# Weights split once in the first stage, with the order of the gap and of the end rearranged

## The reference

```python
x = x + layernorm(attn(layernorm(x)))
x = x + layernorm(ffn(layernorm(x)))

def attn(X):
    h = layernorm(X) * ln_w + ln_b
    Q, K, V = split(h @ W_in + b_in, 3)
    Q, K = rope_half(Q), rope_half(K)
    A = sum(K / norm(K) * V, over the tokens of a batch)
    return (A[:, None, :] * Q) @ W_out + b_out + X

def ffn(x):                      # 8 experts, H = 256; shared SH = 512
    gates = softmax of the top 2 of x @ gate_w
    routed = sum over e of gates[e] * (gelu(x @ w1[e] + b1[e]) @ w2[e] + b2[e])
    return routed + gelu(x @ shared_w1 + shared_b1) @ shared_w2 + shared_b2
```

## Time and profile before

| what | value |
|---|---|
| median of 3 runs | 1030.75 us (1030.19 to 1032.58) |
| the profiled execution | 1027.98 us |
| its span, first to last instruction | 1025.8 us |
| TensorE busy | 896.8 us, 87% |
| VectorE, ACT, GpSimd busy | 628.3, 442.0, 404.4 us |
| mean granted TensorE clock | 0.95 |
| first stage | about 0 to 316 us |
| second stage | 316 to 540 us |
| gap | 540 to 657 us |
| routed tiles | 657 to 910 us |
| last stage | 910 to 1026 us |

### The profile page before, as it was taken

How to read it: one execution, slowest core, us unless ns; L and a number is a source line. 1 busy time by engine, 2 the same in 40 slices (tenths; PEclk the granted TensorE clock), 3 DMA queues, 4 the chain that set the end, 5 groups by cost and what they waited for, 6 DMA issues and landing times.

```text
span 1025.8 us, 14729 instructions
## 1 busy us (share of the span) xinstructions
PE 896.8 (87%) x4562; PEld 739.3 (72%) x4562; DVE 628.3 (61%) x1356; ACT 442.0 (43%) x830; POOL 404.4 (39%) x337
## 2 busy tenths in 40 slices
PE   1999999999997699999999748499999999969883
PEld 1877787787785467777778537488988988857662
DVE  5656766676664775656665587366665666655653
ACT  4134233433423124122242645366666666653462
POOL 3356446545631400000000000277677777730464
PEclk9999999999998889999999878799999999989886
DMA  9122644545337568645424650678778878789496
GB/s 314 45 81 105 244 143 161 188 158 200 135 144 306 190 239 312 227 165 215 154 83 169 215 151 32 238 144 149 140 147 163 154 146 149 147 176 350 62 160 107
DMA packets 78074, 174.68 MB, mean 170 GB/s; under 512 B 10841, under 2 KB 19289, under 8 KB 73137
## 3 DMA queue, kind: packets, MB, share of 16 engines
q1 hardware_dynamic: 52096, 124.60, 33.6%
q0 software_dynamic: 20592, 45.96, 25.1%
q10 hardware_dynamic: 5312, 3.18, 1.3%
HBM read 103.68 MB, written 80.53 MB: 180 GB/s over the span
## 4 chain that ended last, share of the span: by engine, by line
PE 70%; DVE 11%; issue 7%; ACT 4%; POOL 3%; DMA 2%; SPq 1%; POOLq 0%; ACTq 0%; DVEq 0%
PE bank L1434 12%; PE bank L1435 12%; PE bank L1436 12%; PE bank L1626 3%; PE bank L1628 3%; PE bank L1627 3%; PE bank L1643 3%; PE bank L1645 3%; PE bank L1644 3%; PE bank L1613 3%; PE bank L1429 3%; POOL out L1413 2%; DVE we L1061 2%; PE bank L1635 2%; ACT hb L535 1%
## 5 line engine op out<-in xcount | busy, mean ns | idle before, releaser
L1385 POOL DMA_INDIRECT f_scratch<-ro,dst x71 | 113.2, 1595 | 48.7 <-SPq L513 23.2
L1377 POOL DMA_INDIRECT xr<-n_scratch,ids x72 | 71.1, 987 | 90.9 <-issue 65.6
L1434 PE MATMUL bank<-wkv_hi,h_hi 128*128 128x512 f32 x256 | 101.1, 395 | 3.8 <-issue 3.8
L1436 PE MATMUL bank<-wkv_hi,h_lo 128*128 128x512 f32 x256 | 100.7, 393 | 0.0
L1435 PE MATMUL bank<-wkv_lo,h_hi 128*128 128x512 f32 x256 | 100.6, 393 | 0.0
L1188 DVE TENSOR_TENSOR ro<-bank,b2b 128x512 f32<-128x512 f32 x71 | 49.1, 692 | 70.3 <-PE bank L1645 70.3
L1626 PE MATMUL bank<-we,x_hi 128*128 x284 | 86.4, 304 | 0.0
L1628 PE MATMUL bank<-we,x_lo 128*128 x284 | 80.7, 284 | 0.0
L1627 PE MATMUL bank<-we,x_hi 128*128 x284 | 80.6, 284 | 0.0
L544 ACT ACTIVATE sq<-kb 128x512 f32<-128x512 f32 x32 | 20.3, 633 | 134.2 <-DVE kb L845 134.2
L1344 POOL TENSOR_TENSOR zr<-zv,half 128x4 f32<-128x4 f32 x8 | 8.1, 1009 | 137.7 <-DVE zv L961 137.7
(11 more groups left out here) (232 smaller groups left out, 2514.2 us busy)
## 6 DMA issues: line engine op xcount, KB each, us to landing
xg<-in_X SPq DMA_DIRECT2D x16, 1024.0 KB, 9.1
q_scratch<-qh SPq DMA_DIRECT2D x8, 1024.0 KB, 3.9
q_scratch<-qb SPq DMA_DIRECT2D x8, 1024.0 KB, 7.1
expert_scratch<-in_w SPq DMA_DIRECT2D x16, 512.0 KB, 7.1
q_hi<-q_scratch SPq DMA_DIRECT2D x8, 1024.0 KB, 4.7
q_lo<-q_scratch SPq DMA_DIRECT2D x8, 1024.0 KB, 6.9
out<-z SPq DMA_DIRECT2D x8, 1024.0 KB, 5.1
n_scratch<-n SPq DMA_DIRECT2D x8, 1024.0 KB, 6.4
```

The lines of the kernel that those rows point to most:

```text
L1377: pool.indirect_dma_start(xr[u][:, :], None, n3_dram, bass.IndirectOffsetOnAxis(ids[:, i:i + 1], 0)).then_inc(row_in[u], 16)
L1385: pool.indirect_dma_start(f_dram, bass.IndirectOffsetOnAxis(dst[:, i:i + 1], 0), ro[i % NRO][:, :], None, compute_op=ALU.add).then_inc(r_s ...
L1434: pe.matmul(dst, hi(k), w_hi(k), start=(k == 0), stop=False)
L1436: last = pe.matmul(dst, lo(k), w_hi(k), start=False, stop=(k == KD - 1 and not more))
```

## The change

- All weights are split in the first stage. `units` lists 20 pieces of 128x1024: two for each expert, two halves for each shared weight. Four are done in each of groups 1 to 5. SP loads a piece into the buffer of its lo part (`load_unit`, three buffer pairs), ACT makes hi (`unit_hi`), VectorE lo (`unit_lo`), and SP stores both (`store_unit`). The copies DRAM to DRAM go. ACT and VectorE spread the four over the group, two in the k and v part, two around q.
- The bias row `bo` is split in group 0, and the bias product takes the constant `ones_f` instead of `bo_one`. `W_out` is loaded behind the last unit, and batch 0 is scaled at g = 6 instead of 4.
- `split_s` at s = 0 goes; the shared weights are loaded as two parts, those of w1 ahead of s = 0 and those of w2 in it.
- EARLY becomes (0, 2, 4, 6, 7), LATE (1, 3, 5). `fill` starts at s = 1 and has seven entries, so that `shared_h(6)` runs in s = 7.
- For s = 7 VectorE does nothing else between `z_moments` and `x2_shift` but the x2 tiles and one `hs_lo_part`; `top2(6)` comes behind the `hs_lo_part` of group 6.
- In the gap no expert is split. The weights are loaded in two parts, some already in s = 3 and 4. `shared_o(7)` runs twice ahead of the one-hot loop and twice in it. `f_out` of group 6 has four buffers of its own.
- The loads of n3 of the first late group and of the shared w1's hi part wait for eight turns of routed tiles. The first late group's four turns have four banks and run among the last routed tiles. `late_h(0)` does the products with hi weights of all four columns first, then those with lo weights, whose transfer is issued behind the last routed product.
- The early groups' f tiles are measured and normalized earlier, f is loaded in another order, each group with its own semaphore; in the last stage nc parts come ahead of statistics. The last late group's x2 is loaded (`x2c`), added by VectorE, and stored by SP without accumulation. One gather and one x turn fewer.

The core of the diff:

```diff
-EARLY = (1, 3, 5, 6, 7)
+EARLY = (0, 2, 4, 6, 7)
...
+        UW = KD * H
+        UG = 4
+        units = [(e, i, 0) for e in range(E) for i in range(2)] + [(E + i, 0, h) for i in range(2) for h in range(2)]
+        UB = 3
...
-        fill = {2 + i: (("h", "o")[i % 2], EARLY[i // 2]) for i in range(6)}
+        fill = {1 + i: (("h", "o")[i % 2], EARLY[i // 2]) for i in range(7)}
...
-        measured = beside((0, 0, 0, 0, 1, 1, 1, 1, 2, 2, 2, 2, 1, 1, 0, 0, 2, 2, 1, 1, 0, 0, 0, 0))
-        normed_in = beside((0, 0, 0, 0, 0, 0, 0, 0, 0, 1, 1, 1, 2, 2, 2, 2, 1, 1, 1, 1, 2, 1, 1, 1))
+        measured = beside((0, 0, 2, 2, 1, 1, 1, 1, 2, 2, 2, 2, 1, 1, 1, 1) + (0,) * 8)
+        normed_in = beside((0, 0, 0, 0, 0, 0, 2, 2, 0, 0, 1, 1, 2, 2, 2, 2, 1, 1, 1, 1, 1, 1, 0, 0))
...
+            def load_unit(u):
+                if u >= len(units):
+                    return
+                if u >= UB:
+                    sp.wait_ge(w_stored[u % UB], 32 * (u // UB))
+                w, k = unit_in(u)
+                sp.dma_start(w_lo[u % UB][:, :].bitcast(F32).rearrange("p (k h) -> p k h", k=k), w).then_inc(raw_w_in[u % UB], 16)
+
+            def store_unit(u):
+                sp.wait_ge(unit_split, u + 1)
+                for c, w in ((0, w_hi), (1, w_lo)):
+                    sp.dma_start(unit_out(u, c), w[u % UB][:, :].bitcast(F32)).then_inc(w_stored[u % UB], 16)
...
             for g in range(NG):
+                u = UG * (g - 1)
+                with_units = 0 <= u < len(units)
                 sp.wait_ge(h_normed, g + 1)
                 load_x(g + 2)
+                if with_units:
+                    store_unit(u)
+                    load_unit(u + 2)
                 if g >= 1:
                     store_q(g - 1)
+                if with_units:
+                    store_unit(u + 1)
+                    load_unit(u + 3)
                 if g + 1 < NG:
                     sp.wait_ge(k_rotated, GT * (g + 1))
                     load_rt(g + 1)
+                if with_units:
+                    store_unit(u + 2)
+                    load_unit(u + 4)
+                if g + 1 < NG:
                     sp.wait_ge(q_rotated, g + 1)
                     load_rf(g + 1)
-                if 1 <= g <= 4:
-                    copy_expert(2 * g - 2)
-                    copy_expert(2 * g - 1)
...
+                if with_units:
+                    store_unit(u + 3)
+                    load_unit(u + 5)
...
-            for n, g in enumerate(f_loads):
-                sp.dma_start(f[g][:, :, :], f_groups[g]).then_inc(f_in[n // 2], 16)
-            sp.wait_ge(stored, 16 * NT)
+            load_f(EARLY[0])
+            load_f(EARLY[1])
+            load_f(LATE[0])
+            load_f(EARLY[2])
+            load_f(EARLY[3])
+            load_n3(2)
+            load_f(LATE[1])
+            load_f(EARLY[4])
+            load_f(LATE[2])
+            sp.dma_start(x2c[:, :, :], out_groups[LATE[2]]).then_inc(f_in[LATE[2]], 16)
+            for j in range(GT):
+                sp.wait_ge(y_added, j + 1)
+                sp.dma_start(out_tiles[GT * LATE[2] + j], f[LATE[2]][:, j, :]).then_inc(late_stored, 16)
...
+            def unit_hi(u):
+                act.wait_ge(raw_w_in[u % UB], 16 * (u // UB + 1))
+                if u >= UB:
+                    act.wait_ge(w_stored[u % UB], 32 * (u // UB))
+                act.activation(w_hi[u % UB][:, :], w_lo[u % UB][:, :].bitcast(F32), ACT.Copy).then_inc(unit_hi_done, 1)
...
+            def unit_lo(g, j):
+                u = UG * (g - 1) + j
+                if 0 <= u < len(units):
+                    dve.wait_ge(unit_hi_done, u + 1)
+                    dve.tensor_tensor(w_lo[u % UB][:, :], w_lo[u % UB][:, :].bitcast(F32), w_hi[u % UB][:, :].bitcast(F32), ALU.subtract)\
+                       .then_inc(unit_split, 1)
...
                 kv_prod(g, 0)
+                unit_lo(g, 0)
                 v_tile(g, 1)
...
                 kv_prod(g, 2)
+                unit_lo(g, 1)
                 v_tile(g, 3)
                 kv_prod(g, 3)
+                unit_lo(g, 2)
                 rotate_q(g)
                 if g + 2 < NG:
                     front_stats(g + 2)
-                if g == GB + 1:
+                unit_lo(g, 3)
+                if g == GB + 2:
                     wo_lo_parts(0)
...
-            expert_lo((5, 1, 2, 6))
...
-                x_turn(i + 1, 1 - u, (i + 1) % NX)
+                if i < PRE:
+                    x_turn(i + 1, 1 - u, (i + 1) % NX)
+                else:
+                    pe.wait_ge(n3c_in[0], 16)
+                    pe.wait_ge(xt_free, PRE)
+                    late_turn_part(0, 0)
                 h_of(i, u, e)
+                if i == PRE:
+                    late_turn_part(0, 1)
                 o_of(i - 1, 1 - u, e_before)
+            pe.wait_ge(th_free, 2 + PRE)
+            late_turn_part(0, 2)
             h_turn(PRE, PRE % 2)
             o_of(PRE, PRE % 2, e)
+            late_turn_part(0, 3)
```

## The result

The changed kernel takes 993.36 us (median of 4 runs, 993.01 to 995.51) where the kernel before, run beside it, takes 1030.47 us: a ratio of 0.9641, 95% interval 0.9621 to 0.9661. It is faster by 37 us. The forecast was 971 us, 59.5 us faster, with a range up to 992: the direction is right, the gain is 1.6 times too large, and the time lies just outside the range.

What follows compares the result with a forecast made beforehand. TensorE bounds first-stage groups and routed tiles; gains lie in its waits between. First stage +4, second-stage start -18, its groups -2, routing -20, late groups -24 make -60 us: 968 profiled, 971 median; range 958 to 984, with A, B, D 955 to 992.

Steps and rivals of the forecast that it cites:

- The new wait for q(1): Start of the second stage: TensorE waits about 3 us for `load_q(1)`, then three `attend` follow.
- The wait ahead of `late_o(0)`: Last stage: VectorE measures two tiles of the first f before `hc_lo(0,3)`; a new wait of some 6 us.
- rival C: First stage: a unit's chain on three buffers sets the pace; +74 instead of +4 us, 1041 us; chance 0.03.
- D: Rival, routing gap: the splits were not on the path; -6 instead of -20 us, 985 us; chance 0.05.
- its own signs: Groups 1 to 5 at 37 us, first `n3` turn about 347, first mark about 591, `late_o(1)` waits under 2 us.
- Rival B: Late stage stays bound by transfers: -10 instead of -24 us, 985 us; chance 0.08.
- From there two waits shrink ... TensorE ends at about 994: Last stage: waits of 4.4 us on `nc_lo` and 3.45 us on `hc_lo` shrink; TensorE's end gains 15 us.
- The groups of the second stage keep their period.: Second stage: group period unchanged, shared products only start one group earlier; -2 us for the `n_lo` wait.
- start of the second stage: From the first stage's end to the first `n3` turn: -18 us, or -14 if q(1) lands 4 us late.
- 0.8 us a group: First stage: first unit's subtraction delays the last k tile and `hb`; five groups, +4 us.
- Rival A: First stage: each subtraction collides with its GpSimd neighbour; some +14 instead of +4 us, 981 us; chance 0.14.
- I count 22: Routing: the marks' loop over 16 batches falls from 29 to 22 us, -7 us.

Runs made afterwards that it cites:

- e3: Changed kernel with two VectorE statistics moved, so none of f is measured ahead of `hc_lo(0,3)`: ratio 0.9642 to the kernel before, last stage 88.3 us.
- e11: Changed kernel with output products of the second and third late group waiting for each `hc_lo` quarter separately: ratio 0.9628 to the kernel before.
- e7: Changed kernel with e3's start, plus ACT normalizations and two VectorE statistics moved behind the gelu: ratio 0.9648 to the kernel before.
- e1: Changed kernel with the stores of zeros issued one group earlier: 984.66 us, ratio 0.9607 to the kernel before.
- e4: Changed kernel without the units' 20 ACT copies and 20 VectorE subtractions, all transfers kept: ratio 0.9586 to the kernel before.
- e8: Changed kernel with the second unit's subtraction left out in each of five groups: ratio 0.9625 to the kernel before.
- e5: Changed kernel with the first two subtractions moved behind the last k/v product, each unit's load ahead of the previous store: ratio 0.9724 to the kernel before.
- e6: Changed kernel with `load_q(1)` issued ten us earlier, ahead of the last q store: ratio 0.9667 to the kernel before.
- a1: Changed kernel repeated without edit, on the same chip as a repeat of the kernel before: span 990.5 us, routed tiles 257.5 us.

## Why the prediction was off

*What held.* The bias row and the splits gone from the gap: marks begin 9.9 us earlier within the gap (forecast 9), the gathers take 3.9 us less (4). The tail: 9.2 us (9). The new wait for q(1), 3.7 us (3). The wait ahead of `late_o(0)`: 7.7 us (6), and `late_h(1)` starts 36.4 us behind the last routed product (36). Rivals C and D did not come: ACT waits for no raw weights, and the marks follow at once. The routed tiles are unchanged. Of its own signs the forecast missed three: the first n3 turn came at 353.2 us instead of 347, the first mark at 600.4 instead of 591, and the wait ahead of `late_o(1)` was 2.14 us, over its 2. Rival B came halfway: last stage and tail gave 16.6 us, between its 10 and the forecast's 24, with f's landing ahead of `late_o(0)` and that of `c_lo` behind it (e3); but the larger part of what is missing is no transfer.

*The step that failed most: "From there two waits shrink ... TensorE ends at about 994".* It counted the last stage's second half nearly free of waits and of slow clock. From `late_h(1)` to the end it took 54.9 us instead of 48. There were 4.4 us of waits for `hc_lo`, 0.7 for `hsc` and slow products behind each. The last quarter's gelu, copy and subtraction (0.67 + 0.63 + 0.69 us) come behind the last `late_h` product, and nothing of the group's own can run beside them as long as TensorE asks for all four quarters. e11 shows this for 4.4 of the 6.9 us; e7 rules out the order of the normalizations; beside the 2.5 that stay, e11's rows have waits for `hsc` (1.7 us) and `f` (1.1). With the first half right, the stage gave 7.4 us of 15.

*"The groups of the second stage keep their period."* They did not: 36.1 us once instead of 30.3. I followed the shared products when they moved a group earlier, but not their stores, and so not past the four transfers of zeros that stand in SyncE's queue in that group. e1 prices it at 6 us.

*The slow clock behind a wait that I had predicted.* I put in 3 us for q(1) but let the three `attend` behind it run at full clock (10.1 us); they took 12.96 us. Term: start of the second stage, -12.7 instead of -16.

*First stage: "0.8 us a group".* Measured 1.5, and 7 us in all with e4. The chain that the forecast priced, first subtraction, last k tile, `hb`, is there, but TensorE's wait for `hb` grows by 0.3 us only (0.43 to 0.72). What the forecast did not count is the wait of 1.1 us for `qb`, most of it due to the second unit's subtraction, ahead of the last v tile (e8: 0.8 us a group). Rival A described the collision and named `h_lo`, but priced four equal ones at 14 us in all. The costly one is the second unit's, and it reaches `h_lo` through `rn`, `acc` and `prod`. By the Trainium skill (SBUF — State Buffer, Who interferes with whom) a VectorE instruction with two SBUF inputs contends with a GpSimd instruction that reads SBUF. By that rule, the trace agrees: even the 128 x 1 `rn` grows from 0.55 to 1.37 us, and in e5 `acc` and `h_lo` grow although VectorE was idle there before.

*The marks' loop: "I count 22".* It took 25.3 us on VectorE (600.4 to 625.7): two output products stand ahead of the first marks on TensorE, which is ready for them only at 606.6, and the last five batches run at the lower clock (12 products in 3.03 us where 12 take 1.42). Read from the timeline, not tried.

The differences of measured and forecast, in the order of the table's rows: 2.8 (the first two), 3.3, 4.3, 2.2, 0.1, then 5.5 for the routed tiles, which before and after share on one chip, 7.6, and -0.2 for the tail: 25.7 us before rounding, the 60 less the 34.3.

*Two slips in the prediction's working.* The units of a group are four transfers of 0.5 MB in and eight out, not "8 transfers to SBUF"; the 6.3 MB are right. And rival C would decide earlier than it says: four units on three buffers take 36 us as soon as a chain takes 27, that is at 12.4 us a landing and not at 17. The landings were far below it, 5.3 us for the loads of the experts' units and 2.6 and 4.1 for their stores (medians).

## What to carry to other kernels

An idle stretch of VectorE is free for work with two SBUF inputs only if GpSimd is idle too: ask what GpSimd does there before moving such work into it. When work moves a step earlier in a hand-written order, walk each of its transfers past everything that its queue holds in the new place. Count slow products behind every wait of some 3 us on TensorE, also one that you predict yourself, and as a risk behind one of 2 us; a wait that ends in another one of the same length has won nothing (e6). And read an experiment's gain from the groups that it changes, not from a stretch that ends in something else (e8).

## What the runs showed of the hardware

The same instructions of the routed tiles took 253.2 to 254.3 us on one chip and 257.5 to 258.3 us on three others, and those of the kernel before 252.6 us once and 257.0 once; 10 to 14 late `hc` against 1 or 2 go with it. A 4 us difference between two profiles of this kernel in that stage is not evidence of a change.

A short wait brings the lower level of the clock at one time and not at another. Behind 3.29 us (e6) the turn's transposes take 1.97 us, at the lower level. Behind 1.78 us, five times in e5, the clock falls three times and stays twice. Behind 2.14 to 2.26 us ahead of an output product it falls in the profiled changed kernel, where 48 products take 12.7 and 12.8 us, and in e7; behind 2.16 us in one of its repeats (a1) and behind 2.26 us in e3 it does not, and the 48 take 11.2 us.
